# Experts' rows scattered to token order burst by burst, by a row number that each row carries, instead of a gather at the end

## The chip, the cores and the metric

One Trainium2 chip, one core. The metric is the device time of one execution in microseconds, the median of the runs. One core has five engines that run side by side, each through its own list of instructions in order: TensorE (PE), VectorE (DVE), ScalarE (ACT), GpSimd (POOL) and SyncE (SP, which here only issues DMAs). They wait for each other by semaphores.

## What is computed

Input x is 8 batches x 512 tokens x 128. The reference, cut to what matters:

```python
xn = _layernorm(x)
# attention, 16 heads of 8, keys and values through a latent of 64, rope, a mask by pages of 32
q = xn @ wq;  lat = xn @ w_down;  k = lat @ wk_up;  v = lat @ wv_up
s = (softmax(mask(rope(q) @ rope(k) / sqrt(8))) @ v) @ wo
# experts: the two best of 8 for each token
logits = silu(t @ rw1 + rb1) @ rw2 + rb2
vals, idx = top_k(logits, 2)
w = softmax over the two, 0 elsewhere
eh = silu(t @ ew1[e] + eb1[e]);  eo = eh @ ew2[e] + eb2[e]
y = t + sum over e of w * eo
out = x + s * silu(y)
```

All is 32-bit. A token's two expert rows are the only ones that are computed: tokens are sorted into tiles by expert.

## The kernel before

**Attention** goes batch by batch (8), and in a batch by groups of four heads (4), 32 groups in all. For a group SyncE copies the rotated queries and keys into `q_stack` and `k_stack` (`stack`, L515), VectorE and ScalarE mask the keys by head (`k_head`), TensorE computes scores once for their maxima only (L652), VectorE reduces them (`row_max`, L994) and negates them, TensorE turns them (L659), ScalarE copies them to `rows` (`neg_max_t`, L826), and SyncE copies these into spare rows of `q_stack` (L535). Then the scores are computed again with the maximum taken off (L670, L673, L674), in three steps of a group; ScalarE takes the exponentials (`probs`, L845), TensorE multiplies by the values (`pv`, L690, into `wide`), which counts `pv_done`: 12 steps a batch. At a group's end ScalarE copies `wide` to `o_cols` (L852). Behind a batch come transposes (L702, L709), the output projection (L716) and a store to `s_rows`.

**Experts.** The routing (VectorE) gives each token's two places in 39 tiles of 256 rows, sorted by expert. GpSimd scatters the normalised rows `xn` to their places in DRAM (`scatter`, L1175, 64 indirect DMAs of 128 rows, three to a chunk, each chunk held until some step of `pv`). The tiles are then taken in ten bursts of four: SyncE loads expert weights and rows of a tile (`load`, L547 and L549) into a ring of eight, TensorE turns the rows (`slots_in`, L726), ScalarE changes its function table, TensorE and ScalarE compute the first layer (L735, L877), ScalarE changes the table back, TensorE and VectorE compute the second layer (L745, L1112) into `y_out`, and SyncE stores it (`store_rows`, L555) to `y_rows`, in the order of the places. When the last burst is stored, GpSimd gathers each token's two rows (`gather`, L1188, 64 indirect DMAs), VectorE adds them with their weights to `xn` (`combine`, L1124, eight operations a batch), ScalarE takes the gate (`gate`, L883), and VectorE makes the result (`result`, L1135 and L1137) from it, the attention's output and x, which SyncE has fetched again (`fetch`).

**The order of the work** is set by a planner that runs when the kernel is built. `agenda` lists every step with a due place (in groups of attention, from the table AT), its engine, an assumed cost and what it comes after; `program` walks through time and gives each engine the step that can start first among the next LOOK ones of its list. The PSUM banks (7, in `ring`) are given out there as well. The steps' functions then issue their instructions in that order and hold the semaphore waits. GpSimd takes its steps strictly in order of their places.

```python
def chunk(kind, place, first, c, *after):
    add(place, "pool", (kind, c, 0), 1.27 * len(chunk_of(c)), (pv_at(first + c), 0.2), *after)
```

At the start GpSimd makes some constants, computes `rstd` of the first batch (L1162) when VectorE has its variances, and then clears `v_cols` and `pair_in` (L1193, L1194). VectorE normalises the first batch (`norm`, L957) behind `rstd`.

## Time and profile before

| | us |
|---|---|
| median of 3 runs | 509.48 (507.35 to 511.65) |
| the profiled execution | 506.21 |
| its span (first to last instruction) | 504.40 |
| TensorE busy in the span | 439.9 |
| VectorE busy | 375.9 |
| ScalarE busy | 339.1 |
| GpSimd busy | 135.4 |

The profile is of one execution. The span is what lies between its first and last instruction, and the execution is 1.81 us longer. Busy time is added up over the whole span and says nothing of where the engines wait for each other; views of a stretch, the waits and the chain of waits do. A row of the timeline has the start, the duration, engine, line and operation, what is written and read, and in brackets how long the engine had stood idle and what ended that. The matmuls are of 32-bit numbers, and each is shown as two or more instructions.

### The profile page before, as it was taken

To read this page: it belongs to the slowest core of one execution; us is meant where nothing else is said; L and a number is where in the kernel's file an instruction comes from. 1 tells how busy PE (TensorE), PEld (TensorE's weight loads), DVE (VectorE), ACT (ScalarE), POOL (GpSimd) and SP (SyncE) were. 2 spreads that over 40 slices of the span, in tenths; PEclk is the share of its full clock that TensorE was granted. 3 is DMA by queue.
4 is the path that set the end of the run, shared out by engine and by line. 5 is a ranking of instruction groups with operands and counts; after the bars stand their busy time and mean duration, and the time that the engine had idled before them with its cause. 6 is when DMAs were issued, how large, how long until landed. Compare 5 with 4: busy or idle time off the path is not lost.

```text
span 504.4 us, 8192 instructions
## 1 busy us (share of the span) xinstructions
PE 439.9 (87%) x2935; PEld 295.2 (59%) x2935; DVE 375.9 (75%) x721; ACT 339.1 (67%) x537; POOL 135.4 (27%) x143
## 2 busy tenths in 40 slices
PE   2659997989999998999999999999999987998371
PEld 1326654455556556777778876786875743664140
DVE  6788986899888987764658565568468898697751
ACT  2068585656767775788877888787886765665760
POOL 4040000156777750000000000000000377667710
PEclk9858998999999999999999999999999998898787
DMA  6643708122332337655565475466212149335423
GB/s 159 177 122 125 259 24 206 40 75 85 97 97 92 106 97 204 165 153 148 144 183 148 134 188 163 134 179 174 76 43 56 48 116 254 90 79 181 130 65 104
DMA packets 65440, 64.54 MB, mean 128 GB/s; under 512 B 11096, under 2 KB 49112, under 8 KB 64888
## 3 DMA queue, kind: packets, MB, share of 16 engines
q1 hardware_dynamic: 54384, 47.89, 35.0%
q0 software_dynamic: 4096, 8.40, 5.7%
q10 hardware_dynamic: 6920, 7.74, 5.0%
q8 instruction: 23, 0.38, 0.3%
q14 instruction: 17, 0.14, 0.1%
HBM read 32.27 MB, written 21.24 MB: 106 GB/s over the span
## 4 chain that ended last, share of the span: by engine, by line
PE 64%; DVE 11%; DMA 7%; SPq 6%; ACT 6%; issue 4%; POOL 1%; DVEq 0%; POOLq 0%; ACTq 0%
PE ring L652 12%; PE wide L690 12%; PE ring L670 9%; PE ring L745 6%; PE ring L735 6%; DMA q_stack<-rows 4%; DVE row_max L994 4%; ACT probs L845 3%; PE ring L673 3%; PE ring L609 3%; PE ring L702 3%; PE ring L674 2%; PE ring L716 2%; PE ring L726 1%; SPq L546 1%
## 5 line engine op out<-in xcount | busy, mean ns | idle before, releaser
L994 DVE TENSOR_REDUCE row_max<-ring 128x4 f32<-128x512 f32 (+2 forms) x192 | 193.5, 1040 | 50.8 <-PE ring L652 50.1
L845 ACT ACTIVATE probs<-ring 128x768 f32<-128x768 f32 (+1 forms) x192 | 163.0, 880 | 75.6 <-PE ring L670 48.0
L1188 POOL DMA_INDIRECT pair_in<-y_rows,place x64 | 61.7, 964 | 238.8 <-PE wide L690 221.1
L652 PE MATMUL ring<-k_head,q_stack 108*128 108x512 f32 (+1 forms) x352 | 114.5, 420 | 4.3 <-ACT probs L845 2.3
L670 PE MATMUL ring<-q_stack,k_head 128*128 128x512 f32 (+1 forms) x256 | 81.8, 418 | 22.0 <-DMA q_stack<-rows 16.8
L690 PE MATMUL wide<-probs,v_cols 128*32 128x512 f32 (+3 forms) x1024 | 89.6, 449 | 1.3 <-ACT probs L845 1.3
L1175 POOL DMA_INDIRECT slot_rows<-xn,place x64 | 62.3, 974 | 88.8 <-PE wide L690 70.6
L652 PEld LDWEIGHTS ring<-k_head,q_stack 108*128 108x128 f32 x352 | 59.1, 194 | 36.2 <-ACT probs L845 16.9
L670 PEld LDWEIGHTS ring<-q_stack,k_head 128*128 128x128 f32 x256 | 45.3, 202 | 45.4 <-DMA q_stack<-rows 18.9
L837 ACT ACTIVATE k_head<-k_stack,hmask 128x512 fp32r<-128x512 f32 x64 | 43.6, 715 | 6.1 <-DMA k_stack<-roped_lo 6.0
L989 DVE TENSOR_SCALAR k_head<-k_stack,hmask 128x512 fp32r<-128x512 f32 x64 | 29.8, 492 | 21.9 <-DMA k_stack<-roped_lo 21.9
L690 PEld LDWEIGHTS wide<-probs,v_cols 128*32 128x32 f32 x1024 | 24.2, 109 | 34.7 <-issue 23.2
L877 ACT ACTIVATE work<-ring,area 128x256 f32<-128x256 f32 x78 | 30.5, 475 | 11.4 <-PE ring L735 11.4
L745 PEld LDWEIGHTS ring<-area,work 128*128 128x128 f32 x312 | 36.4, 192 | 1.4 <-ACT work L877 0.8
L745 PE MATMUL ring<-area,work 128*128 128x128 f32 x312 | 36.9, 276 | 0.2 <-DVE row_max L994 0.2
L735 PE MATMUL ring<-slots_t,area 128*128 128x256 f32 x156 | 36.6, 384 | 0.1
L673 PE MATMUL ring<-q_stack,k_head 128*128 128x256 f32 x128 | 36.1, 310 | 0.4 <-ACT probs L845 0.2
L673 PEld LDWEIGHTS ring<-q_stack,k_head 128*128 128x128 f32 x128 | 24.2, 189 | 19.2 <-issue 7.3
L735 PEld LDWEIGHTS ring<-slots_t,area 128*128 128x128 f32 x156 | 28.7, 190 | 7.5 <-ACT slots_t L868 2.1
L674 PE MATMUL ring<-q_stack,k_head 128*128 128x256 f32 x128 | 32.4, 281 | 0.0
L762 ACT ACT_TABLE_LOAD x25 | 32.1, 1283 | 0.4
L852 ACT COPY o_cols<-wide 128x512 f32<-128x512 f32 x32 | 18.6, 582 | 12.7 <-PE wide L690 12.0
(131 smaller groups left out, 456.4 us busy)
## 6 DMA issues: line engine op xcount, KB each, us to landing
area<-w_pack SPq DMA_DIRECT2D x39, 321.0 KB, 3.0
area<-slot_rows SPq DMA_DIRECT2D x39, 128.0 KB, 3.1
y_rows<-work SPq DMA_DIRECT2D x39, 128.0 KB, 2.7
k_stack<-roped_hi SPq DMA_DIRECT2D x64, 64.0 KB, 2.0
slot_rows<-pair_in ACTq DMA_DIRECT2D x4, 1024.0 KB, 4.5
q_stack<-roped_hi SPq DMA_DIRECT2D x64, 64.0 KB
k_stack<-roped_lo SPq DMA_DIRECT2D x32, 64.0 KB, 2.0
q_stack<-roped_lo SPq DMA_DIRECT2D x32, 64.0 KB
```

The costliest lines, as they stand in the source:

```text
L652: last = mm(ps[:, k, 0:each * width].rearrange("p (c w) -> p c w", c=each), q_stack[0:MAX0, g, i * P:(i + 1) * P], k_head[0:MAX0, r:r + ea ...
L670: last = mm(ps[:, r, j * P:T], k_head[:, h, j * P:(j + 1) * P], q_stack[:, g, j * P:T], start=True, stop=True)
L673: mm(ps[:, r, 0:2 * P], k_head[:, h, 3 * P:T], q_stack[:, g, 2 * P:T], start=True, stop=True)
L674: last = mm(ps[:, r, 2 * P:T], k_head[:, h, 2 * P:3 * P], q_stack[:, g, 2 * P:T], start=True, stop=True)
L690: last = mm(wide[32 * r:32 * r + 32, dst:T], v_cols[:, tile, GH * g + r, :], probs[:, n % 2, r, src:src + T - dst], start=(tile == 0), sto ...
L735: last = mm(ps[:, c % 2, f * ROWS:(f + 1) * ROWS], w_ring[:, BURST * (burst % 2) + c, f * P:(f + 1) * P], slots_t[:, c * ROWS:(c + 1) * RO ...
L745: last = mm(ps[:, 0, (c % 2) * ROWS + a * E:(c % 2) * ROWS + (a + 1) * E], hidden[:, c, f, a * P:(a + 1) * P], w_ring[:, BURST * (burst % ...
L837: activation(k_head[:, h, :], k_stack[:, g, :], ACT.Copy, scale=hmask[:, r:r + 1]).then_inc(heads_act[g], 1)
L845: activation(probs[:, n % 2, 2 * half:2 * half + 2, lo:T], ps[:, :, lo:T], ACT.Exp, scale=SCALE).then_inc(exp_done, 1)
L994: reduce(row_max[:, g, i, heads[0]:heads[-1] + 1].rearrange("p (a c) -> p a c", c=each), ps[:, :, 0:each * (i + 1) * P].rearrange("p a (c ...
L1175: G.indirect_dma_start(slot_rows, bass.IndirectOffsetOnAxis(ap=place[:, which, t:t + 1], axis=0), xn[:, t, :], None).then_inc(scattered, 16)
L1188: G.indirect_dma_start(pair_in[:, b % 2, which, t * E:(t + 1) * E], None, y_rows, bass.IndirectOffsetOnAxis(ap=place[:, which, at:at + 1], ...
```

## The change

- Each row of `xn` gets a 129th number, the row of `y_rows` to which the expert's result is to go: token number + 9984 (NSLOT) for a token's first expert, and 4096 more for its second. Two iota operations of GpSimd make the numbers. The scatters carry it along: rows are now 516 B, and the order is all first places, then all second ones; between them GpSimd waits until the first 32 scatters have landed and adds 4096 in place.
- The scatters are held for later steps of attention: the first chunk until step 12 (before, 10).
- When a burst's rows are loaded, VectorE takes the maximum of the carried number and the slot's own number (`where`): rows that nobody filled have 0 there and go to their own slot, which nobody reads.
- A burst's results are no longer stored by SyncE but sent by GpSimd (`send`): eight indirect DMAs of 128 rows a burst, 78 in all, to rows in token order. The next burst's second layer waits for them, as it waited for the stores.
- There is no gather. SyncE loads a batch's rows with two plain DMAs of 256 KB (`pairs`), behind the last send.
- The bursts are due 1.553 groups apart instead of 1.0, other places in the table AT are new, LOOK is 28 instead of 16. Two rules are added to the planner: ScalarE's table isn't changed while its held banks leave no pair free, and TensorE starts no other work for ScalarE while the other table is loaded.
- GpSimd clears `v_cols` and `pair_in` ahead of the first batch's `rstd`, not behind it.

```diff
-          pv=0.73, stats=-9.37, route=2.12, scatter=3, burst=(13.14, 1.0), load=0.66, gather=24)
-LOOK, DRIFT = 16, 0.02
+          neg=-0.979, pv=0.862, stats=-9.37, route=3.002, scatter=11 / 3, burst=(12.892, 1.553), load=-0.067,
+          pairs=(30.71, 0.736))
+LOOK, DRIFT = 28, 0.02
...
-                drain_after=[(("sp", ("store_rows", i - 1, 0)), 2.0)] if i else ())
-        add(at + 0.2, "sp", ("store_rows", i, 0), 0.65 * len(tiles), (("dve", ("layer2", i, 1)), 0.1))
+                drain_after=[(("pool", ("send", i - 1, 0)), 2.2)] if i else ())
+        add(at + 0.2, "pool", ("send", i, 0), 2.54 * len(tiles), (("dve", ("layer2", i, 1)), 0.1), (("dve", ("where", i, 0)), 0.1))
...
+            if step[0] == "silu_table" and step[1] < NBURST:
+                kept = {i for other, by in held.items() if by == "act" for i in place[other]}
+                if all({i, i + 1} & kept for i in range(NBANK - 1)):
+                    continue
             if e == "pe" and step in drain:
+                if silu is not None and silu[1] < NBURST and drain[step] == "act" and step[0] != "layer1":
+                    continue
...
-        xn = sb("xn", [P, BT, E])
+        xn = sb("xn", [P, BT, ROW])
...
-        slot_rows = dram("slot_rows", (NTILE * ROWS, E))
-        y_rows = dram("y_rows", (NTILE * ROWS, E))
+        slot_rows = dram("slot_rows", (NSLOT, ROW))
+        y_rows = dram("y_rows", (NSLOT + 2 * B * T, E))
...
-            def store_rows(burst, _):
-                sp.wait_ge(y_ready, 2 * burst + 2)
-                for k in tiles_of(burst):
-                    sp.dma_start(y_rows[ROWS * k:ROWS * k + ROWS, :].rearrange("(a p) d -> p a d", p=P),
-                                 y_out[:, k % BURST, :, :]).then_inc(y_stored, 16)
+            def pairs(b, _):
+                if b == 0:
+                    sp.wait_ge(y_stored, 32 * NTILE)
+                if b >= 2:
+                    sp.wait_ge(mixed, b - 1)
+                for which in range(2):
+                    at = NSLOT + (B * which + b) * T
+                    sp.dma_start(pair_in[:, b % 2, which, :].rearrange("p (t e) -> p t e", e=E), y_rows[at:at + T, :].rearrange(
+                        "(t p) e -> p t e", p=P)).then_inc(pairs_in[b % 2], 16)
...
+            def where(burst, n):
+
+                for k in tiles_of(burst):
+                    dve.wait_ge(w_in_ring[k % W_RING], 32 * (k // W_RING) + 32)
+                count, at = len(tiles_of(burst)), BURST * (burst % 2)
+                if burst >= 2:
+                    dve.wait_ge(y_stored, 32 * BURST * (burst - 1))
+                tt(goes_to[:, at:at + count, :], slots[:, at:at + count, :, E].bitcast(I32),
+                                slot_no[:, BURST * burst:BURST * burst + count, :], ALU.max).then_inc(where_ready, 1)
...
-                pool.wait_ge(pv_done, 3 * AT["scatter"] + c + 1)
-                for t, which in (divmod(k, 2) for k in chunk_of(c)):
+                pool.wait_ge(pv_done, round(3 * AT["scatter"]) + c + 1)
+                for which, t in (divmod(k, BT) for k in chunk_of(c)):
+                    if which and t == 0:
+                        pool.wait_ge(scattered, 16 * BT)
+                        G.tensor_scalar(xn[:, :, E].bitcast(I32), xn[:, :, E].bitcast(I32), BT * P, None, ALU.add).then_inc(named, 1)
+                        pool.wait_ge(named, 2)
                     G.indirect_dma_start(slot_rows, bass.IndirectOffsetOnAxis(ap=place[:, which, t:t + 1], axis=0),
                                          xn[:, t, :], None).then_inc(scattered, 16)
...
-            row_stats(0, 0)
+            def send(burst, n):
+
+                pool.wait_ge(where_ready, burst + 1)
+                pool.wait_ge(y_ready, 2 * burst + 2)
+                for k in tiles_of(burst):
+                    for a in range(2):
+                        G.indirect_dma_start(y_rows, bass.IndirectOffsetOnAxis(ap=goes_to[:, k % W_RING, a:a + 1], axis=0),
+                                             y_out[:, k % BURST, a, :], None).then_inc(y_stored, 16)
+
             G.memset(v_cols[:], 0.0).then_inc(prep_pool, 1)
             G.memset(pair_in[:], 0.0).then_inc(prep_pool, 1)
-            walk("pool", {"stats": row_stats, "scatter": scatter, "gather": gather})
+            row_stats(0, 0)
```

How the instructions stand now. The line numbers of the changed kernel are higher (L826 is L838 there, L845 L857, L852 L864, L883 L895, L762 L774).

ScalarE around the last group of attention, before: `probs` are exponentials, `xn<-xn` the gates, `rows<-ring` the copy of the last maxima.

```order
L845 ACTIVATE probs<-ring 128x1024 x2
L845 ACTIVATE probs<-ring 128x2x384 x4
L762 ACT_TABLE_LOAD
L762 ACTIVATE table_out<-table_in 128x1
L883 ACTIVATE xn<-xn 128x512 x6
L762 ACT_TABLE_LOAD
L762 ACTIVATE table_out<-table_in 128x1
L826 COPY rows<-ring 32x128
L852 COPY o_cols<-wide 128x512
L845 ACTIVATE probs<-ring 128x1024 x2
L845 ACTIVATE probs<-ring 128x2x384 x4
L762 ACT_TABLE_LOAD
```

ScalarE at the same place, changed:

```order
L857 ACTIVATE probs<-ring 128x1024 x2
L857 ACTIVATE probs<-ring 128x2x384
L838 COPY rows<-ring 32x128
L857 ACTIVATE probs<-ring 128x2x384 x3
L864 COPY o_cols<-wide 128x512
L857 ACTIVATE probs<-ring 128x1024 x2
L857 ACTIVATE probs<-ring 128x2x384 x4
L774 ACT_TABLE_LOAD
L774 ACTIVATE table_out<-table_in 128x1
L895 ACTIVATE xn<-xn 128x4x128 x6
L774 ACT_TABLE_LOAD
L774 ACTIVATE table_out<-table_in 128x1
L864 COPY o_cols<-wide 128x512
```

The copy of the last maxima (L838) moved ahead of the six gates and ahead of the three exponentials that end the group before; the gates and both table loads moved behind the last exponentials.

GpSimd at its start, before: `steps` and `tile_no` are constants.

```order
L1152 IOTA steps 128x16
L1154 IOTA tile_no 128x39
L1162 TENSOR_TENSOR rstd<-var_eps,half_exp 128x4
L1193 MEMSET v_cols 128x2048
L1194 MEMSET pair_in 128x2048
L1162 TENSOR_TENSOR rstd<-var_eps,half_exp 128x12
```

GpSimd at its start, changed:

```order
L1174 IOTA steps 128x16
L1176 IOTA tile_no 128x39
L1214 MEMSET v_cols 128x2048
L1215 MEMSET pair_in 128x2048
L1184 TENSOR_TENSOR rstd<-var_eps,half_exp 128x4
L1217 IOTA slot_no 128x78
L1218 IOTA xn 128x32
L1184 TENSOR_TENSOR rstd<-var_eps,half_exp 128x12
```

The two memsets moved ahead of the first `rstd`, and two iota operations came behind it.

TensorE around the last burst of the experts, before: L726 turns the burst's rows, L735 and L745 are its two layers.

```order
L726 MATMUL ring<-ident,area 128x128 x6
L652 MATMUL ring<-k_head,q_stack 128x512 x2
L609 MATMUL ring<-x_col,w_att 128x512
L735 MATMUL ring<-slots_t,area 128x256 x6
L652 MATMUL ring<-k_head,q_stack 128x512 x3
L690 MATMUL wide<-probs,v_cols 32x512 x4
L745 MATMUL ring<-area,work 128x128 x8
L659 MATMUL ring<-ident,neg_max 32x128
L745 MATMUL ring<-area,work 128x128 x4
```

TensorE around the last burst, changed (L738, L747 and L757 are the same three):

```order
L671 MATMUL ring<-ident,neg_max 32x128
L738 MATMUL ring<-ident,area 128x128 x6
L702 MATMUL wide<-probs,v_cols 32x384 x4
L664 MATMUL ring<-k_head,q_stack 128x384 x2
L747 MATMUL ring<-slots_t,area 128x256 x6
L664 MATMUL ring<-k_head,q_stack 128x384 x2
L702 MATMUL wide<-probs,v_cols 32x256 x4
L702 MATMUL wide<-probs,v_cols 32x128 x4
L757 MATMUL ring<-area,work 128x128 x12
L682 MATMUL ring<-q_stack,k_head 128x512 x4
```

The burst itself is the same; before, 1,542 matmuls stand ahead of it, now 1,772, and the transposes of maxima that follow it (L659, now L671) are eight before and four now. Ahead of the first burst stand 778 matmuls before and 786 now.

## Rows read from the trace of the kernel before

**Rows 1.** The page, part 1: busy us, share of the span, instructions
```profile
PE 439.9 (87%) x2935; PEld 295.2 (59%) x2935; DVE 375.9 (75%) x721; ACT 339.1 (67%) x537; POOL 135.4 (27%) x143
```

**Rows 2.** Busy time in stretches; columns: length, each engine, granted clock, DMA share, GB/s
```profile
200.00:400.00 200.00, 198.00 (x1402) 147.77 (x1402) 130.19 (x218) 159.37 (x261) 1.82 (x2) 1.00 0.51 136
400.00:471.00 71.00, 61.81 (x426) 36.84 (x424) 59.31 (x115) 43.29 (x61) 52.04 (x55) 0.93 0.48 134
471.00:479.50 8.50, 0.09 (x2) 0.01 (x1) 7.30 (x16) 5.68 (x12) 6.37 (x8) 0.65 0.60 170
```

**Rows 3.** The page, part 5: groups; busy, mean ns, idle before and its releaser
```profile
L994 DVE TENSOR_REDUCE row_max<-ring 128x4 f32<-128x512 f32 (+2 forms) x192 | 193.5, 1040 | 50.8 <-PE ring L652 50.1
...
L745 PE MATMUL ring<-area,work 128*128 128x128 f32 x312 | 36.9, 276 | 0.2 <-DVE row_max L994 0.2
L735 PE MATMUL ring<-slots_t,area 128*128 128x256 f32 x156 | 36.6, 384 | 0.1
```

**Rows 4.** Timeline of TensorE at 375 us; columns: start us, us, instruction
```profile
375.41 1.06 PE L745 MATMUL ring<-area,work 128*128 128x128 f32 x8
```

**Rows 5.** Waits of 400 to 487 us: us in total, times, longest
```profile
PE ring L670 <- DMA q_stack<-rows: 12.4, 3, 8.4
```

**Rows 6.** Timeline of ScalarE from 470 to 477 us
```profile
469.97 1.28 ACT L762 ACT_TABLE_LOAD   x1
...
471.38 3.21 ACT L883 ACTIVATE xn<-xn 128x512 f32<-128x512 f32 x6
...
476.01 0.24 ACT L826 COPY rows<-ring 32x128 f32<-32x128 f32 x1
```

**Rows 7.** The chain of waits in order of time: start us, us, what
```profile
184.12 2.23 DMA slot_rows<-xn,place
...
194.00 0.44 SPq L549
...
422.23 5.02 DMA q_stack<-rows
...
476.54 2.90 DMA q_stack<-rows
...
486.59 1.28 ACT L762
...
500.96 0.69 DVE area L1137
```

**Rows 8.** Timelines of the start, the normalisations' row to 10.6 and to 10.2 us
```profile
5.41 1.05 POOL L1162 TENSOR_TENSOR rstd<-var_eps,half_exp 128x4 f32<-128x4 f32 x1 [4.02 <-DVE var_eps L950]
...
6.49 4.13 DVE L957 TENSOR_SCALAR xn<-area,mean,rstd 128x128 f32<-128x128 f32 x4 [1.17 <-POOL rstd L1162]
...
6.49 3.87 DVE L957 TENSOR_SCALAR xn<-area,mean,rstd 128x128 f32<-128x128 f32 x3 [1.17 <-POOL rstd L1162]
...
8.16 1.79 POOL L1194 MEMSET pair_in<- 128x2048 f32 x1
```

**Rows 9.** Timeline of GpSimd: the tenth and the last scatter
```profile
115.17 0.96 POOL L1175 DMA_INDIRECT slot_rows<-xn,place  x1 [4.88 <-PE wide L690]
...
184.12 0.96 POOL L1175 DMA_INDIRECT slot_rows<-xn,place  x1 [0.30 <-issue]
```

**Rows 10.** The page, part 6: DMA issues, KB each, us to landing
```profile
area<-slot_rows SPq DMA_DIRECT2D x39, 128.0 KB, 3.1
```

**Rows 11.** Timeline of TensorE: the first burst's transposes
```profile
205.76 1.04 PE L726 MATMUL ring<-ident,area 128*128 128x128 f32 x8
```

**Rows 12.** Groups of VectorE, from 99 to 183 and from 200 to 390 us
```profile
L989 DVE TENSOR_SCALAR k_head<-k_stack,hmask 128x512 fp32r<-128x512 f32 x16 | 7.7, 505 | 0.7 <-DMA k_stack<-roped_lo 0.7
...
L989 DVE TENSOR_SCALAR k_head<-k_stack,hmask 128x512 fp32r<-128x512 f32 x21 | 9.6, 483 | 19.2 <-DMA k_stack<-roped_lo 19.2
```

**Rows 13.** Busy time from 420 to 430 us, columns as in rows 2
```profile
420.00:430.00 10.00, 6.12 (x44) 3.54 (x43) 8.12 (x17) 4.93 (x8) 7.76 (x8) 0.96 1.01 288
```

**Rows 14.** Timeline of VectorE: the first combine
```profile
411.49 2.31 DVE L1124 SCALAR_TENSOR_TENSOR xn<-pair_in,pair_w,xn 128x128 f32<-128x128 f32 x8
```

More of the change, by code:

```diff
@@ L184, in agenda @@
     for c in range(NCHUNK):
-        chunk("scatter", AT["scatter"] + c / 3, 3 * AT["scatter"], c, *([(("dve", ("places", 0, 0)), 0.1)] if c == 0 else []))
-        chunk("gather", AT["gather"] + c / 3, 3 * AT["gather"], c,
-              *([(("sp", ("store_rows", NBURST - 1, 0)), 2.5)] if c == 0 else []),
-              *[(("dve", ("combine", b - 2, 0)), 0.1) for b in range(2, B) if 2 * TT * b in chunk_of(c)])
+        chunk("scatter", AT["scatter"] + c / 3, round(3 * AT["scatter"]), c, *([(("dve", ("places", 0, 0)), 0.1)] if c == 0 else []))
     for i in range(NBURST):
@@ L192, in agenda @@
             add(at - AT["load"] + 0.1 * (k % BURST), "sp", ("load", i, k), 1.3, (("pool", ("scatter", NCHUNK - 1, 0)), 2.5),
-                *([(("pe", ("layer2", i - 2, 1)), 0.2)] if i >= 2 else []))
+                *([(("pe", ("layer2", i - 2, 1)), 0.2), (("dve", ("where", i - 2, 0)), 0.1)] if i >= 2 else []))
+        add(at, "dve", ("where", i, 0), 0.25, *[(("sp", ("load", i, k)), 3.5) for k in tiles])
         job(at, ("slots_in", i, 0), 0.22 * len(tiles) + 0.05, "act", 0.22 * len(tiles) + 0.17,
@@ L211, in agenda @@
     for b in range(B):
-        add(AT["gather"] + last_chunk(b) / 3 + 0.7, "dve", ("combine", b, 0), 2.4, (("pool", ("gather", last_chunk(b), 0)), 2.2),
+        add(AT["pairs"][0] + AT["pairs"][1] * b, "sp", ("pairs", b, 0), 1.3, (("pool", ("send", NBURST - 1, 0)), 2.2),
+            *([(("dve", ("combine", b - 2, 0)), 0.1)] if b >= 2 else []))
+        add(AT["pairs"][0] + AT["pairs"][1] * b + 0.3, "dve", ("combine", b, 0), 2.4, (("sp", ("pairs", b, 0)), 2.5),
             (("dve", ("weights", 0, 0)), 0))
@@ L545, in load @@
                     sp.wait_ge(y_ready, 2 * burst - 2)
+                    sp.wait_ge(where_ready, burst - 1)
                 expert = sp.value_load(tile_e[0:1, k:k + 1], min_val=0, max_val=NE - 1)
@@ L578, in result @@
                 sp.dma_start(out[b].rearrange("(t p) e -> p t e", p=P), s_all[:, TT * b:TT * b + TT, :]).then_inc(stored, 16)
-            walk("sp", {"stack": stack, "neg": maxima, "load": load, "store_rows": store_rows, "s_out": s_out,
+            walk("sp", {"stack": stack, "neg": maxima, "load": load, "pairs": pairs, "s_out": s_out,
                         "fetch": fetch, "result": result})
@@ L801, in norm @@
                 for t in range(TT * b, TT * b + TT):
-                    last = activation(xn[:, t, :], x_all[:, t, :], ACT.Identity, scale=rstd[:, t:t + 1],
+                    last = activation(xn[:, t, 0:E], x_all[:, t, :], ACT.Identity, scale=rstd[:, t:t + 1],
                                       bias=shift[:, t:t + 1])
@@ L1109, in layer2 @@
                 if burst >= 1:
-                    dve.wait_ge(y_stored, 16 * BURST * burst)
+                    dve.wait_ge(y_stored, 32 * BURST * burst)
                 for c in halves_of(burst, q):
@@ L1143, in _ @@
                          "logits": logits, "top": top_two, "gap": gap, "count": count, "ranks": ranks, "places": places,
-                         "weights": weights, "layer2": layer2, "combine": combine, "result": result})
+                         "weights": weights, "where": where, "layer2": layer2, "combine": combine, "result": result})
         @block.gpsimd
```

46 lines of the change are left out of this document (20 added, 26 removed).

## The prediction

> **What bounds the kernel now.** I read the page's shares first: TensorE is busy for 87% of the span, VectorE for 75%, ScalarE for 67% [rows 1]. That averages over stages with different limits, so the next view is the busy time in stretches [rows 2]. From 200 to 400 us, where experts and attention are mixed, TensorE is busy for 198.0 of 200 us: nothing that other engines save there shortens the kernel. Its idle time lies later: 9.2 us between 400 and 471, and all of 471 to 479.5. The experts' two layers are 73.5 us of matmuls [rows 3], and they are used up by 377 us [rows 4]; behind that only attention is left to fill TensorE. The waits of 400 to 487 us name the largest holes: the score matmuls waited three times, 12.4 us together and 8.4 us at the longest, for the copy of the negated maxima into q_stack [rows 5]. ScalarE's timeline tells why [rows 6]: at 469.97 it loads a table, then runs six gates of finished batches, loads the other table, and only at 476.01 copies the last group's maxima (`rows`), behind which SyncE's copy (2.90 us to land, [rows 7]) and the last scores stand.
>
> **The start.** VectorE's four normalisations of the first batch take 4.13 us from 6.49 on, the first three of them 3.87 us, so the fourth adds 0.26 [rows 8]. Beside them GpSimd runs two memsets of 1.79 us, until 9.95. The change issues the memsets ahead of the `rstd` operation that releases the normalisations. GpSimd had stood idle for 4.02 us ahead of that operation [rows 8], from 1.39 to 5.41, so the two memsets (3.6 us) end by 5.0. The four operations should then cost 4 x 0.26 = 1.0 us, and the stage ends 3.1 us sooner. Small operations of VectorE just ahead may meet a memset's end; I charge 0.3 us. Everything up to the first scores hangs on this chain: I take -2.8 us, bounds -3.1 and 0 (if a later load takes over the wait).
> The Trainium skill ("SBUF — State Buffer", section "SBUF: two separate sides") says that a VectorE instruction in a two-port mode and a GpSimd instruction exclude each other for the whole instruction. By that rule the full gain is real, and the trace agrees: of the four, the slow ones lie beside the memsets and the last one, behind them, takes 0.26 us more.
>
> **The rows' scatter.** Of the 64 scatters the last 55 start every 1.27 us from 115.17 to 184.12, behind a 4.88 us wait for TensorE [rows 9]; nine stood ahead of it. The new limits (the 12th step of attention instead of the 10th, then one more step per three scatters) leave three there, so six more come behind 115.17: +7.6 us. Between the halves GpSimd now waits for its DMAs to land, 2.23 us for the last [rows 7], and adds 4096 to the row numbers. No row shows that operation; between nothing and the 1.05 us of `rstd` [rows 8] I take 0.4, and 0.3 for the restart: +2.9 us. The last scatter starts 10.5 us later, 2.8 of it given back by the start: 191.8, landed at 194.1. Before, SyncE had issued the fourth tile's loads 8.1 us behind the landing (184.12 + 2.23 to 194.44, [rows 7]), and they landed 3.1 us later [rows 10]: now 205.3. In TensorE's order the first burst stands behind nearly the same work as before (786 matmuls against 778), so TensorE is there at 205.76 [rows 11] - 2.8 + 0.5 = 203.5. It stands still for 1.8 us; since the landing is a median and the burst needs the fourth tile last, I take +1.5, bounds 0 and +5. Rows of 516 B instead of 512: no row shows such a load; the 3.1 us of the 512 B rows stands, and later loads are issued a burst ahead.
>
> **Stores, gathers, sends.** 39 store issues leave SyncE and 64 gathers leave GpSimd; 78 sends come. At the scatters' 1.27 us the eight of a burst take 10.2 us, and the bursts now stand further apart (ten in some 220 us, 22 us each). A send reads y_out before the next burst's results overwrite it: 10.2 + 2.2 us against 22, so that wait is covered, and if it weren't, VectorE would hold the results and TensorE's banks. Ten `where` operations of 128x8 are each below the 0.69 us of a 128x512 operation [rows 7], on a VectorE that is busy for 130 of 200 us there [rows 2]. Beside DMAs of GpSimd, VectorE's k_head operations take 505 ns, without them 483 [rows 12]: +0.02 us each, hidden too. All at 0; the bounds are 0 and what the third rival costs.
>
> **The spread bursts.** The last burst now stands behind 1,772 matmuls instead of 1,542: four groups of attention are left behind the experts, not eight. A burst is 7.4 us of the two layers (a tenth of 73.5) and 1.0 of transposes [rows 11]. Three of them now lie behind 385 us and fill TensorE's holes up to 430 us, of which 3.9 us lie between 420 and 430 [rows 13] and 1.6 before. I take -5.0 us, bounds -9.2 (all idle time from 400 to 471 us) and 0.
>
> **The last groups.** ScalarE now copies the last maxima ahead of the last group's exponentials, and the gates stand behind all of them. The hole of 8.4 us goes. What is late next is the way behind the last exponentials, which end at 486.6 [rows 7]: table load, the copy of `o_cols`, transposes, projection, store, fetch, the last result, 17.8 us to the end. Now six gates (3.21) and a second table load with its small operation (1.41, from 469.97 to 471.38) stand before that copy [rows 6]: +4.7. VectorE has four results (two operations of 0.69 us each, [rows 7]) ahead of `out_rows`; the first can start 2.0 us behind the exponentials, so they end at about 7.6, as the first transposes do: +0.2. Bounds of this part: -8.4 + 3 and -4 + 7 (if that copy still lands late).
>
> **Sum.** Span 504.4 - 2.8 + 1.5 - 5.0 - 8.4 + 4.7 + 0.2 = 494.6 us. Around the span lie 506.21 - 504.40 = 1.81 us: 496.4. The profiled execution stood 0.65% under the median of the runs (509.48), so 496.4 x 509.48 / 506.21 = **499.6 us**. All bounds at once give spans of some 487 and 512 us, that is 492 and 517 by the same factor.
>
> **Rivals.**
> *Loads collide with the copies of maxima.* One such copy took 5.02 us to land behind a series of 256 KB fetches, another 2.90 [rows 7]. The change puts sixteen loads of 256 KB (`pairs`) into the last 60 us, where 64 gathers had spread the same bytes. If the last batch's four copies each land 3 us later and nothing hides it, 12 us come back: span 506.6, **511 us**. For it: a DMA share of 1.01 from 420 to 430 us [rows 13]. Against: VectorE's maxima run ahead of the copies.
> *The clock stays up.* TensorE's granted clock is 0.93 from 400 to 471 us and 0.65 in the hole behind it, against 1.00 from 200 to 400 [rows 2]: part of the time at the lower of its two levels. If the denser work keeps the upper level, some 5 us (0.07 of 71) and the other 4.2 us of idle time go as well: span 485, **490 us**.
> *The sends are slow, and the kernel slower than before.* They run beside VectorE's work, and each burst's results wait for the previous sends; the 220 us of the bursts leave 2.8 us for each of 78. If each were held up by nearly two of VectorE's reductions (1.04 us, [rows 3]) it took 3.1 us, and they would end at 213 + 242 = 455, land and be loaded by 461. Then VectorE has two combines (2.31 us each, [rows 14]), eleven maxima (1.04) and the negations before the last group can be scored, 17 us; then scores and sums 11, and the tail of 22.7: span 512, **517 us**. It decides from about 2.5 us a send. Against it: the scatters kept 1.27 us beside a VectorE with little idle time.
> The Trainium skill speaks for this rival: "SBUF — State Buffer", section "SBUF: two separate sides", warns that DMAs issued by GpSimd are starved of descriptors while VectorE works in a mode that takes the shared ports, which would put this kernel on this rival's side. The scatters' even spacing doesn't bear that out, so its chance is small.
>
> **How the numbers follow.** Forecast as summed 0.66 (494 to 504 us), clock 0.12, collisions 0.15, slow sends 0.07. One per cent, 5 us, is about what a measurement of this kernel can tell from no change. Faster by over 1% (under 504.4): 0.66 and 0.12, so 0.78. Within 1%: what is between, taken as the collisions, of which some part comes back at nearly every size: 0.15. Slower: 0.07. The range goes from the clock case to the full collisions, 490 to 511 us.
>
> **What would show each step.** The four normalisations at 1.0 to 1.4 us; a gap of some 3 us in the middle of the scatters and a last one near 192; a first burst near 205 us with a short hole ahead; sends every 1.27 us; experts' matmuls until about 425 us; no hole of TensorE over 4 us in the last batch; six gates behind the last exponentials, and some 22.7 us from these to the end. Copies into q_stack that land after 4 to 5 us, or sends over 2.5 us apart, would make the forecast wrong; a first part that is no shorter would take 2.8 us from it.

## The result and the profile after

The changed kernel takes 528.26 us, median of four runs (524.55 to 534.08), the kernel before on the same chip 508.42 (four runs, 506.10 to 511.65): ratio 1.036, 95% interval 1.024 to 1.049. It is slower by 20 us; the forecast was 499.6 and faster. The profiled execution is the longest of the four, 534.08 us with a span of 532.3; counts of waits and places of holes are read from it, times from the medians. Medians are of all runs, ratios leave out runs that lie over 1.5% above the fastest of their kernel, as the profiled one does.

The page of the changed kernel, parts 1 and 6 (to set beside [rows 1, 10]), with the sends' group of part 5:

```profile
PE 458.5 (86%) x2935; PEld 310.5 (58%) x2935; DVE 372.6 (70%) x731; ACT 337.7 (63%) x537; POOL 152.7 (29%) x160
...
L1211 POOL DMA_INDIRECT y_rows<-work,goes_to x78 | 76.6, 982 | 191.7 <-DVE work L1134 170.2
...
area<-w_pack SPq DMA_DIRECT2D x39, 321.0 KB, 3.4
area<-slot_rows SPq DMA_DIRECT2D x39, 129.0 KB, 4.2
```

The load of a tile's rows lands after 4.2 us, where the forecast kept the 3.1 us of the 512 B rows [rows 10]. In the experiments with rows of 516 B it is 3.3 to 4.4 us, in the one with 512 B 3.5, so that the rows' size does it is not shown; and a kernel of the experiments with 3.9 us was as fast as the kernel before, so this isn't the loss.

Busy time in stretches of the changed kernel, columns as in [rows 2]:

```profile
200.00:400.00 200.00, 178.52 (x1170) 127.62 (x1169) 116.02 (x203) 129.44 (x209) 54.81 (x56) 0.93 0.46 129
400.00:471.00 71.00, 67.14 (x476) 49.23 (x475) 44.29 (x69) 52.80 (x86) 21.81 (x22) 0.97 0.36 101
```

TensorE does the same 2,935 matmuls, but from 200 to 400 us, where it had 2.0 us of idle time [rows 2], it now has 21.5, and its granted clock is 0.93 instead of 1.00. The waits of the changed kernel name the place, TensorE's, VectorE's and SyncE's in this order (SPq is SyncE's queue; L682 are the scores, L554 the tile loads, L1134 is layer 2's copy out, L1125 the step `where`):

```profile
PE ring L682 <- DMA q_stack<-rows: 19.7, 8, 4.8
...
DVE work L1134 <- PE ring L757: 33.3, 16, 6.9
...
DVE goes_to L1125 <- DMA area<-slot_rows: 5.9, 3, 2.8
...
SPq L554 <- DVE work L1134: 60.8, 7, 12.6
```

Before, SyncE waited at the loads for layer 2 only 6.2 us in 8 waits; now 60.8 in 7. The kernel before:

```profile
SPq L546 <- DVE work L1112: 6.2, 8, 1.3
```

The chain of waits of the changed kernel from 322 us on shows how one of these waits ends (start us, us, what; four loads follow each other from 325.89 on, the last issue is shown):

```profile
322.36 1.80 PE ring L757 x16
324.19 0.77 DVE work L1134 x2
324.97 0.46 SPq L554
...
325.89 0.35 SPq L555
326.28 0.43 SPq L557
...
331.23 0.44 SPq L557
331.71 4.41 DMA q_stack<-rows
336.17 0.74 PE ring L682 x2
```

Layer 2 of burst i ends; SyncE, which had stood at the first load of burst i+2, issues four tiles' loads (1.65 us a tile); only then comes the copy of the maxima, and it lands 4.41 us later, behind four tiles of 450 KB each. The maxima had been in `rows` since 328.28 us (ScalarE's copy, L838), so 3.4 us went by in SyncE's queue, behind loads that its long wait had pushed to this place. TensorE stands still for 3.2 us meanwhile. The loaded rows are used only some 20 us later. There are holes that end with a copy of maxima at 276, 333, 366 and 389 us (3.0, 3.2, 2.5 and 4.8 us; the copy of the third stood behind six stack copies that the loads had held up), and TensorE pays for them twice. Stretches of the changed kernel around the last of them:

```profile
380.00:389.00 9.00, 8.94 (x62) 4.73 (x60) 8.18 (x13) 5.06 (x9) 5.00 (x6) 1.00 0.64 174
389.00:394.00 5.00, 0.25 (x1) 0.25 (x2) 2.25 (x6) 0.00 (x0) 2.75 (x3) 0.82 0.85 272
394.00:402.00 8.00, 8.00 (x37) 5.12 (x38) 1.63 (x5) 5.44 (x8) 0.00 (x0) 0.69 0.04 9
402.00:410.00 8.00, 8.00 (x56) 6.71 (x56) 3.73 (x5) 6.79 (x14) 0.00 (x0) 1.00 0.01 2
```

Behind the 4.8 us hole the granted clock is 0.69 for 8 us, part of them at the lower of the two levels: TensorE is busy all the time and gets 37 matmuls done where the next 8 us hold 56. The two mixes differ, so the counts alone don't give the price; matmuls of one shape do: the first four score matmuls behind the hole (L682, 128x512) take 670 ns each, where the mean over the kernel is 471, and the next eight value products (L702, 128x512) 951 ns, where it is 639. In this way busy time rises from 439.9 [rows 1] to 458.5 us in the profiled executions with no matmul more; the mean granted clock is 0.917 there, before 0.952.

### The profile page after: what moved, and what is told of

The parts are those of the page before. It is cut to its first block, busy times and chain, and to the rows that moved or that the text cites. A ratio compares the mean times of both kernels' runs of the same rounds, so it can differ in the third digit from the quotient of the medians.

```text
span 532.3 us, 8245 instructions
## 1 busy us (share of the span) xinstructions
PE 458.5 (86%) x2935; PEld 310.5 (58%) x2935; DVE 372.6 (70%) x731; ACT 337.7 (63%) x537; POOL 152.7 (29%) x160
## 4 chain that ended last, share of the span: by engine, by line
PE 56%; SPq 13%; DMA 10%; DVE 8%; ACT 7%; issue 3%; POOL 1%; DVEq 0%; POOLq 0%; ACTq 0%
PE wide L702 10%; PE ring L664 10%; PE ring L682 8%; PE ring L747 7%; PE ring L757 6%; DMA q_stack<-rows 5%; ACT probs L857 4%; DMA k_stack<-roped_lo 4%; DVE row_max L1006 3%; SPq L554 3%; SPq L533 2%; SPq L555 2%; SPq L557 2%; PE ring L621 2%; SPq L530 2%
## 5 line engine op out<-in xcount | busy, mean ns | idle before, releaser
L857 ACT ACTIVATE probs<-ring 128x768 f32<-128x768 f32 (+1 forms) x192 | 161.7, 881 | 73.8 <-PE ring L682 60.1
L1211 POOL DMA_INDIRECT y_rows<-work,goes_to x78 | 76.6, 982 | 191.7 <-DVE work L1134 170.2
L664 PE MATMUL ring<-k_head,q_stack 108*128 108x512 f32 (+1 forms) x352 | 119.4, 435 | 7.6 <-ACT probs L857 3.0
L682 PE MATMUL ring<-q_stack,k_head 128*128 128x512 f32 (+1 forms) x256 | 83.9, 429 | 22.1 <-DMA q_stack<-rows 19.7
L1202 POOL DMA_INDIRECT slot_rows<-xn,place x64 | 64.2, 1002 | 101.9 <-PE wide L702 83.6
L702 PE MATMUL wide<-probs,v_cols 128*32 128x512 f32 (+3 forms) x1024 | 90.7, 453 | 0.9 <-ACT probs L857 0.9
L664 PEld LDWEIGHTS ring<-k_head,q_stack 108*128 108x128 f32 x352 | 62.5, 202 | 43.6 <-ACT probs L857 17.5
L682 PEld LDWEIGHTS ring<-q_stack,k_head 128*128 128x128 f32 x256 | 45.7, 205 | 50.1 <-DMA q_stack<-rows 23.5
L702 PEld LDWEIGHTS wide<-probs,v_cols 128*32 128x32 f32 x1024 | 24.2, 110 | 35.4 <-issue 25.3
L747 PE MATMUL ring<-slots_t,area 128*128 128x256 f32 x156 | 38.0, 396 | 1.0 <-ACT slots_t L880 0.9
L1134 DVE TENSOR_TENSOR work<-ring,area 128x256 f32<-128x256 f32 x39 | 14.8, 419 | 33.6 <-PE ring L757 33.3
L757 PEld LDWEIGHTS ring<-area,work 128*128 128x128 f32 x312 | 36.5, 192 | 3.0 <-ACT work L889 1.6
L757 PE MATMUL ring<-area,work 128*128 128x128 f32 x312 | 37.8, 276 | 0.0
L747 PEld LDWEIGHTS ring<-slots_t,area 128*128 128x128 f32 x156 | 29.9, 197 | 9.1 <-ACT slots_t L880 2.4
L864 ACT COPY o_cols<-wide 128x512 f32<-128x512 f32 x32 | 18.7, 586 | 24.0 <-PE wide L702 23.9
```

The lines of the kernel that those rows point to most:

```text
L664: last = mm(ps[:, k, 0:each * width].rearrange("p (c w) -> p c w", c=each), q_stack[0:MAX0, g, i * P:(i + 1) * P], k_head[0:MAX0, r:r + ea ...
L682: last = mm(ps[:, r, j * P:T], k_head[:, h, j * P:(j + 1) * P], q_stack[:, g, j * P:T], start=True, stop=True)
L702: last = mm(wide[32 * r:32 * r + 32, dst:T], v_cols[:, tile, GH * g + r, :], probs[:, n % 2, r, src:src + T - dst], start=(tile == 0), sto ...
L747: last = mm(ps[:, c % 2, f * ROWS:(f + 1) * ROWS], w_ring[:, BURST * (burst % 2) + c, f * P:(f + 1) * P], slots_t[:, c * ROWS:(c + 1) * RO ...
L757: last = mm(ps[:, 0, (c % 2) * ROWS + a * E:(c % 2) * ROWS + (a + 1) * E], hidden[:, c, f, a * P:(a + 1) * P], w_ring[:, BURST * (burst % ...
L857: activation(probs[:, n % 2, 2 * half:2 * half + 2, lo:T], ps[:, :, lo:T], ACT.Exp, scale=SCALE).then_inc(exp_done, 1)
```

## Experiments

Theories: **A**, SyncE's order (loads that wait hold the copies behind them) makes the loss; **B**, the new path itself costs it (sends, wide rows, traffic); **C**, the new table costs it on all engines. Later ones are D to G. The experiments were run in four groups, so a kernel is best compared by its ratio to the kernel before in its own group. The kernel before, run beside them, had medians of 505.4 to 508.4 us.

**Path and table apart.** New path, positions of before:

```diff
+AT = dict(proj=(-1.9, -1.53, -0.34, 1.77, 2.13, -1.16), router=(0.19, 0.04), heads=-1.71, max=-1.29, max_step=0.12, neg=-1.02,
+          pv=0.73, stats=-9.37, route=2.12, scatter=3, burst=(13.14, 1.0), load=0.66, pairs=(24 + 2 / 3 + 0.7, 8 / 3))
+LOOK, DRIFT = 16, 0.02
```

> The new path alone: GpSimd's scatter with a row number in each row, the sends, wide rows, pair loads and the new start, with the table of positions, the look-ahead of 16 and the burst spacing of 1.0 of the kernel before. Theory A (SyncE's order): near the kernel before, 500 to 512 us, since few copies of maxima stand behind loads that wait. Theory B (the new path itself, by its descriptors, its 516-byte rows or its traffic): 520 us or more. Theory C (table): 500 to 512 us, as A.

Measured 527.81 us, ratio 1.042 (1.034 to 1.049). The other half, kernel before with the new positions, LOOK 28 and the planner's two rules (`burst=(12.892, 1.0)`, `gather=24`):

> The table alone: the kernel before, with its row stores and gathers, by the changed kernel's positions and look-ahead of 28; the bursts keep the spacing of 1.0, since the gathers need the last 84 us. Theory A: 505 to 515 us, as the loads stand between the row stores and are fewer ahead of a copy of maxima. Theory B: 500 to 510 us. Theory C (the positions outside the bursts, such as earlier maxima and later value products, cost it on all engines): 518 us or more.

Measured 508.46 us, ratio 0.999 (0.994 to 1.004). By these two alone the path is guilty and the table (in all but the bursts' spacing, which was left at 1.0) free. But the waits of VectorE in the first (new path, old table) show a wait that the changed kernel hardly has (L1124 is `where` there):

```profile
DVE goes_to L1124 <- DMA y_rows<-work,goes_to: 32.2, 8, 7.5
```

`where` of burst i stands in VectorE's order where its loads are due to have landed, well ahead of the burst's layer 2, and waits for the sends of burst i-2 to land; maxima are queued behind it. So it was moved, alone:

```diff
+def where_late(steps):
+    out = []
+    for s in steps:
+        if s[0] == "where" and s[1] >= 1:
+            continue
+        if s[0] == "layer2" and s[1] >= 1 and s[2] == 0:
+            out.append(("where", s[1], 0))
+        out.append(s)
+    return out
+
+
+ORDER["dve"] = where_late(ORDER["dve"])
```

> The kernel with the new path by the old table (527.8 us), with one step moved on VectorE alone: the step that forms a burst's row numbers stands directly ahead of that burst's first layer 2 copy, not behind its loads. Theory D (the path itself is cheap; what cost 20 us there is that this step waits, in VectorE's queue, for the sends of the burst before last: 32.2 us in 8 waits, and the maxima behind it then come late to TensorE, four holes of 3.5 to 5.6 us ahead of layer 1): 500 to 510 us. Theory B (the path costs by its traffic and its descriptors): above 518 us, with the holes still there or with copies landing late.

Measured 503.11 us, ratio 0.996 (0.993 to 0.999): 24.7 us by the medians, some 23 by the ratios, for one step of 0.16 us in another place. Its TensorE from 200 to 400 us, new path, old table, `where` late:

```profile
200.00:400.00 200.00, 197.38 (x1399) 147.78 (x1396) 130.47 (x229) 157.23 (x257) 75.40 (x78) 1.00 0.49 141
```

All 78 sends lie in this stretch (the x78 of GpSimd), and TensorE is as full as before [rows 2]. Theory B has fallen: the path is free, and so is the table at the old spacing; what each lost was lost by order.

**Copies of maxima first.** In the changed kernel, each `neg` ahead of the run of loads directly before it:

```diff
+        if s[0] in kinds:
+            while at and out[at - 1][0] == "load" and out[at - 1][1] >= 2:
+                at -= 1
+        out.insert(at, s)
...
+ORDER["sp"] = neg_first(ORDER["sp"], ("neg",))
```

> The changed kernel (528 us), with one thing moved on SyncE alone: each copy of maxima that stands directly behind loads of tiles (bursts from the third on) is issued ahead of them (3 to 4 loads, 1.65 us of SyncE each, ahead of 4 copies). Theory A (SyncE's queue costs the loss: loads that wait for layer 2 hold the copies of maxima behind them, in the changed kernel's waits SyncE waited 60.8 us for VectorE at the loads, and TensorE 19.7 us in 8 waits for the copies): the holes of 3.0, 3.2, 2.5 and 4.8 us at 276, 333, 366 and 389 us shrink to 1 us or less, 510 to 520 us. Theory B (the path by GpSimd's sends costs it) and theory C (the table of positions costs it on every engine, not by SyncE): 524 us or more.

Measured 526.63 us (ratio 1.039), a miss for A as it was put. The waits of this kernel point to the reason: TensorE's for the copies fell from 19.7 to 10.6 us, but VectorE's at `where` rose from 7.8 us to 19.7 (13.4 for earlier sends, 6.3 for the rows):

```profile
PE ring L696 <- DMA q_stack<-rows: 10.6, 5, 4.9
...
DVE goes_to L1139 <- DMA y_rows<-work,goes_to: 13.4, 3, 4.9
```

With `where_late` on top:

> As the kernel with the copies of maxima first, and VectorE's step that forms the row numbers of a burst moved down its order to stand directly ahead of that burst's first layer 2 copy, so that VectorE no longer waits for the landing of tile loads (5.9 us in 3 waits in the changed kernel). Theory A: 2 to 6 us below the kernel with the copies first alone, since loads that go out later would otherwise hold VectorE. Theories B and C: the same as that kernel within 3 us.

Measured 521.46 us (ratio 1.031), in the range of A. What was left is shown by the chain of waits of a kernel with the same two moves (it comes below, with four): stack copies (L568, L571) stand behind the loads (L593, L595) as well. ScalarE's k_head (L887) waits for them, behind it in ScalarE's order stands slots_t (L918), which layer 1 (L785) reads, and TensorE has a hole of 4.3 us:

```profile
319.94 0.44 SPq L595
320.47 1.26 SPq L568
...
323.05 0.59 SPq L571
323.68 2.95 DMA k_stack<-roped_lo
326.65 1.33 ACT k_head L887 x2
327.99 0.90 ACT slots_t L918
328.94 6.78 PE ring L785 x16
```

**Loads behind every copy that is due within 10 us**, stack copies too:

```diff
+def loads_later(steps, by):
+    return sorted(steps, key=lambda s: DONE["sp", s] + (by if s[0] == "load" and s[1] >= 2 else 0))
+
+
+ORDER["sp"] = loads_later(ORDER["sp"], 10)
```

With `where_late`:

> The changed kernel with row numbers directly ahead of layer 2 (as before) and, on SyncE alone, every tile load of the third burst on moved behind the stack copies and copies of maxima that the plan puts up to 10 us after it; its rows are needed 20 us later. With the copies of maxima alone ahead of the loads it was 521.5 us, and three holes were left that wait for a stack copy queued behind loads. Theory A (SyncE's queue): those holes go too, 512 to 518 us. If the stack copies are late by the traffic of the loads and not by the queue: 520 to 524 us.

Measured 501.93 us, ratio 0.980 (0.970 to 0.991), 26 us below the changed kernel, faster than the kernel before, and 10 us below the range expected by A: the move did more than close the holes that had been counted. TensorE and SyncE in this kernel: the stretch, TensorE's wait for the maxima (L703), and the head of SyncE's waits, where the loads' wait for layer 2 is no longer found:

```profile
200.00:400.00 200.00, 192.04 (x1342) 139.99 (x1339) 129.30 (x222) 147.20 (x238) 62.62 (x64) 0.98 0.51 138
```

```profile
PE ring L703 <- DMA q_stack<-rows: 6.4, 3, 4.0
...
SPq L563 <- ACT rows L859: 102.9, 24, 12.1
SPq L551 <- PE wide L723: 72.0, 21, 11.4
SPq L593 <- ACT s_sb L895: 18.7, 5, 8.3
```

**Which of the two moves?** Each alone, and half the distance:

> The changed kernel with SyncE's order alone altered: every tile load of the third burst on stands behind the copies that the plan puts up to 10 us after it; VectorE's step for the row numbers stays where it was. With both moves the kernel had 501.9 us. Theory A (SyncE's queue alone made the loss): 502 to 508 us. Theory G (the two orders must move together: a load that goes out later holds VectorE, which waits for its landing to form the row numbers, with the maxima queued behind): 512 us or more, and waits of VectorE at the row numbers for slot rows of over 15 us in all, where it was 5.9 us.

> The changed kernel with VectorE's order alone altered: row numbers directly ahead of layer 2, SyncE's order as in the changed kernel. Theory A: 521 to 527 us, since VectorE waited only 7.8 us there and the holes by the copies of maxima stay. If VectorE's wait was a cause of its own: below 519 us.

> As the kernel of 501.9 us, but the loads stand behind copies that the plan puts up to 5 us after them, not 10. Theory A, if it is the few copies directly behind the loads that matter: half or more of the gain, 505 to 514 us, with waits of SyncE for VectorE at the loads between the 60.8 us of the changed kernel and the few of the kernel with 10 us. If the gain came from something else in the order: no step between, near 502 or near 521 us.

| in the changed kernel: us (ratio) | `where` as it was | `where` late |
|---|---|---|
| loads as they were | 528.26 (1.036) | 526.70 (1.035) |
| loads 5 us later | not run | 516.08 (1.010) |
| loads 10 us later | 542.39 (1.059) | 501.93 (0.980) |

The loads alone make it slower still, by 14 us by the medians and some 12 by the ratios. VectorE's first wait in that kernel:

```profile
DVE goes_to L1133 <- DMA area<-slot_rows: 64.0, 9, 11.5
```

`where` waits for the rows' landing; with the loads later it holds VectorE for 64.0 us, in 9 waits, with maxima behind it. So A alone has fallen, and G holds: the loads stood early on SyncE, `where` stood early on VectorE and wanted their rows there, and one of the two queues pays unless both steps move. With `where` late, 5 us give 10.6 of the 24.8 us. That is a step between, but less than the half or more that was expected, and 2 us above the range. SyncE's waits at the loads, for layer 2 and for `where`, are between as well, 25.7 us:

```profile
SPq L575 <- DVE work L1155: 15.8, 3, 7.0
...
SPq L574 <- DVE goes_to L1146: 9.9, 3, 5.9
```

**Start and end.** The second and third zeroing write moved ahead of the fourth:

```diff
+put(ORDER["act"], ("zero", 1, 0), ("zero", 3, 0))
+put(ORDER["act"], ("zero", 2, 0), ("zero", 3, 0))
```

> The changed kernel with one thing moved on ScalarE alone: the second and third zeroing write, which the new table issues right behind the first at 21 us, stand ahead of the fourth, at some 45 us. Theory E (the three writes of 1 MB together delay the stack copies of batch 0: k_stack<-roped_lo landed 4.3 us after its issue, and TensorE's first value product ended at 71.6 us where it was 67.5 us before and 63.2 us with the old table): first value product at 63 to 66 us and 520 to 523 us in all. If the start was lost by something else: 68 us or later, and the same time as the changed kernel.

Measured 522.96 us (520.22 to 524.83; the changed kernel's runs reach down to 524.55, so the total alone says little). The place does: the first value product ends at 63.2 us, 71.6 in the changed kernel. The chain of waits of the changed kernel shows SyncE's issues of the stack copies, of about 0.6 us, getting slow when three 1 MB writes go out from 21.20 on:

```profile
21.41 0.59 SPq L536
...
22.04 1.20 SPq L537
...
23.29 1.48 SPq L530
...
28.01 1.69 SPq L533
...
29.74 4.29 DMA k_stack<-roped_lo
```

The copy of the last outputs ahead of the table load and the gates:

```diff
+put(ORDER["act"], ("o_copy", B - 1, NG - 1), ("silu_table", NBURST, 0))
```

> The changed kernel with one thing moved on ScalarE alone: the copy of the last attention group's outputs stands ahead of the Silu table load and the six gates, not behind them and a further table load. The hole of 5.8 us in TensorE ahead of the last transposes should go, and the gates come 0.6 us later: if the chain through the output projection sets the end, 521 to 524 us; if the results of the batches (gates, VectorE's products, stores) set it, no change within 1.5 us.

Measured 526.88 us (ratio 1.039), no gain. The first hole went, and another of 7.0 us came behind the first transposes, which this kernel's waits put down to VectorE:

```profile
PE ring L729 <- DVE o_rows L1038: 7.0, 1, 7.0
```

From the last value product to the end it is 24.0 us against 24.8: VectorE's combines and results set the end as much as the gates did.

**Put together.**

> All four moves at once in the changed kernel: copies of maxima ahead of loads, row numbers directly ahead of layer 2, zeroing writes later, last output copy ahead of the gates. If the four losses are separate, 521.5 us (the first two) less 4 to 6 (start) less 4 to 6 (end): 510 to 514 us. If they were all one delay that shows at different places, 518 us or more.

Measured 511.73 us (ratio 1.011, 1.006 to 1.016), as expected if the losses are separate.

> The same with the zeroing writes later and the last output copy ahead of the gates. The kernel with the four moves had 511.7 us. Theory A: 503 to 509 us, as TensorE's holes of 2.7, 4.3, 2.8 and 2.2 us at 296, 325, 353 and 403 us go; what stays above 503 us is the end, where VectorE combines after the last exponentials. If the traffic delays the stack copies: 510 to 513 us.

Measured 499.12 us (495.83 to 499.91), ratio 0.976 (0.967 to 0.985): the fastest kernel of the study, ahead of both, and 4 us below the range expected. Against the kernel of 501.93 us the difference is within the spread of that kernel's runs (496.61 to 507.54). TensorE in it from 200 to 400 us:

```profile
200.00:400.00 200.00, 195.63 (x1360) 143.66 (x1360) 132.20 (x230) 151.60 (x246) 62.63 (x64) 0.99 0.50 136
```

**The spacing.** Theory F: it is the wider spacing of the bursts that costs. Changed kernel with `burst=(12.892, 1.0)`, the old table's pair loads, `where` and zeroing writes late; and the other way round, new path, old table, `where` late with the new spacing, load and pair places:

> The new path with the new table in everything but the bursts' spacing (1.0 for 1.553) and the pair loads' places (those of the old table), zeroing writes later, row numbers directly ahead of layer 2. Theory F (the wider spacing is what puts loads ahead of copies, leaves holes and pushes the combines behind the end): 501 to 507 us. If the other positions of the table (maxima, value products, look-ahead of 28) cost it: 512 us or more.

> The other way round: the best kernel so far (503.1 us, new path, old table, row numbers directly ahead of layer 2) with only the burst spacing of 1.553, the load's place and the pair loads' places of the new table. Theory F: 513 to 520 us, holes between the bursts again and a tail of some 24 us behind the last value product. If the spacing is harmless: 503 to 507 us.

Measured 503.11 us (ratio 0.985, 0.977 to 0.994) and 533.28 us (1.045, 1.036 to 1.055). TensorE's waits for the copies of maxima in the two:

```profile
PE ring L703 <- DMA q_stack<-rows: 8.9, 6, 3.7
...
PE ring L695 <- DMA q_stack<-rows: 21.9, 6, 5.8
```

F holds as a condition: at 1.0 the planner's order leaves few loads in the copies' way, at 1.553 many. The new spacing, with the load's and the pair loads' places that were changed beside it, cost 30 us by the medians and some 25 by the ratios, more than expected. The load's place does no harm by itself, since the first of the two kernels has it too. The spacing isn't a cause by itself either, since 1.553 with the loads later had 501.9 and 499.1 us.

## Why the prediction was wrong

**The step that failed.** "Stores, gathers, sends" ended in "All at 0; the bounds are 0 and what the third rival costs", and of the loads it was only said, under the scatter, that "later loads are issued a burst ahead". That is true, and it is the fault: a load issued a burst ahead waits in SyncE's queue for layer 2, and whatever stands behind it waits as well. In the two holes that were followed, at 333 and 389 us, the copies of the maxima stood 3.4 and 4.4 us in the queue behind such loads and landed 1.5 and 2.2 us later than the 2.90 us of [rows 7]. I counted what leaves SyncE (39 stores), not what the remaining loads stand in front of, in an order that a new table had rearranged. In the same way "Ten `where` operations … hidden" priced their time, below 0.69 us each, and not their waits: with the old table these were 32.2 us and cost 24.7 us of the kernel. No rival held this. The missing term, for both orders together, is +26.3 us by the medians (528.26 - 501.93) and 28 by the ratios, and the bounds of the sum did not contain it.

**The spread bursts** (-5.0). TensorE's holes were not filled but moved: it stood still 21.5 us from 200 to 400 where I had counted on 2.0. The bursts did not keep to 22 us each: their sends start some 27 us apart (from 224.67 to 441.18 us for the first nine). The last layer 2 ended at 458.4 us, forecast "until about 425":

```profile
455.42 2.95 PE L757 MATMUL ring<-area,work 128*128 128x128 f32 x24
```

With both orders mended it ended at 430.6 us (the kernel of 501.9 us) and 420.6 (499.1 us). In the second of these TensorE is idle 4.4 us from 200 to 400 and 7.3 from 400 to 471, together 11.7 where it was 2.0 and 9.2 before, so the term was near 0 even there.

**The start** (-2.8). The operation did as forecast:

```profile
6.37 1.12 DVE L969 TENSOR_SCALAR xn<-area,mean,rstd 128x128 f32<-128x128 f32 x4 [1.17 <-POOL rstd L1184]
```

1.12 us against 4.13 [rows 8]. The rule that the forecast had cited from the Trainium skill ("SBUF — State Buffer", section "SBUF: two separate sides"), that a VectorE instruction in a two-port mode and a GpSimd instruction exclude each other, agrees with this. But a later load took over the wait, the bound of 0 that I had named, and more: the first value product ended 4.1 us later than before (71.6 against 67.5). The new table's three zeroing writes in a row were in the change, and I had not gone through ScalarE's DMAs. With them late it ended at 63.2, 4.3 us ahead of before.

**The rows' scatter** (+1.5) held in its size: a hole of 1.46 us ahead of the first burst (1.8 by the dates, 1.5 taken). Its dates were late: the scatters behind TensorE's wait start at 117.27 us where the forecast had 112.4 (115.17 - 2.8), the last one starts at 197.62 (191.8), and the first burst came at 210.96 us (205). The late start explains 4.9 us of the 5.8 at the last scatter.

```profile
197.62 0.96 POOL L1202 DMA_INDIRECT slot_rows<-xn,place  x1 [0.30 <-issue]
```

In the middle two scatters start 3.26 us apart, so the pause adds 2.0 us to their spacing of 1.27. The forecast added 2.9, since its 2.23 us to land were counted from the start of the last scatter, a part of which the spacing holds already.

**The sends** held: 982 ns each, every 1.27 us within a burst, and the third rival's reason is out, though the kernel is slower, as it said. The Trainium skill's warning ("SBUF — State Buffer", section "SBUF: two separate sides") was set against the scatters' spacing for it. Of these 78 sends beside a VectorE that is busy for 58% of the time from 200 to 400 us none takes over 1.49 us, and the median is 967 ns. The warning is of a mode of VectorE, and no trace here shows which operations ran in it, so this is no test of the warning itself.

**The last groups** (-8.4, +4.7, +0.2). The hole of 8.4 us was gone, and the way behind the last exponentials took 25.7 us (506.57 to 532.3) for the 22.7 forecast. Timeline of ScalarE there:

```profile
505.06 1.51 ACT L857 ACTIVATE probs<-ring 128x768 f32<-128x768 f32 x2 [0.48 <-PE ring L686]
...
507.99 3.21 ACT L895 ACTIVATE xn<-xn 128x512 f32<-128x512 f32 x6
...
512.62 0.57 ACT L864 COPY o_cols<-wide 128x512 f32<-128x512 f32 x1
```

The six gates take the 3.21 us counted, the copy of `o_cols` ends 6.6 us behind the exponentials, as forecast, and VectorE's results end as the first transposes do (515.24 us), as the +0.2 had it. The 3.0 us too much lie behind that. The longer way ahead of the transposes is a hole of 5.8 us in TensorE (1.1 before), and behind it the same 28 matmuls of transposes and projection take 6.86 us for 3.78, at the lower level of the clock throughout. Busy time there, the changed kernel and then the kernel before:

```profile
513.24:522.00 8.76, 6.86 (x28) 5.77 (x28) 7.66 (x15) 2.83 (x5) 0.00 (x0) 0.50 0.49 140
...
488.60:494.00 5.40, 3.78 (x28) 3.12 (x28) 3.73 (x10) 1.71 (x3) 0.00 (x0) 1.00 0.05 15
```

The +4.7 priced ScalarE's operations and not the clock of the matmuls behind them; in this kernel the term measured +7.7.

**The rivals.** "Loads collide with the copies of maxima" named the right victim at the wrong place: between 449 and 507 us TensorE had one such hole, of 1.95 us. The collisions were with the tiles' loads of the middle, which existed before, and the queue ahead of the copy did more than the traffic: 3.4 and 4.4 us against 1.5 and 2.2, as above. (By the forecast's own steps this rival's total comes to 511.7 us, not 511.) "The clock stays up" came true where it looked, 0.97 from 400 to 471 us for 0.93, but the clock fell from 1.00 to 0.93 from 200 to 400, where no rival had looked.

That the fastest kernel, at 499.1 us, meets the forecast of 499.6 us is luck in part: the -5.0 us of the spread bursts was near 0 there too. The forecast left out what stands in front of what, and that kernel has little of it; what its 9 us under the kernel before consist of was not taken apart further.

## What to carry to other kernels

In this kernel a step that waited cost what stood behind it in its queue, not its own time. So for every queue that a change reorders, list each waiting instruction with the three or four instructions behind it and who needs those, before anything is called hidden. Prefetches go behind the short copies that the bound engine needs next, as late as their own use allows; and a step that reads the prefetched data must move with them on its own engine, or the wait only changes queues. When both halves of a change look free or guilty by themselves, look at the waits of each, since two orders can trade the same loss.

## What the runs showed of the hardware that I had not expected

- A hole in TensorE is paid twice: after 4.8 us of standing still the granted clock was 0.69 over the next 8 us, and matmuls of 128x512 took 670 and 951 ns there that take 471 and 639 in the mean of the kernel. After 5.8 us of standing still near the end it was 0.50, and the 28 matmuls that took 3.78 us in the kernel before (granted clock 1.00) took 6.86. TensorE's busy time rose by 18.6 us with the matmuls the same.
- Three 1 MB writes issued by ScalarE within 2.4 us came with slow issues of SyncE's copies, 1.2 to 2.1 us each for the 0.6 otherwise, from 22.04 to 31.8 us, and with a 64 KB copy that landed after 4.29 us. With one such write there (the kernel with the other two late), only the issues from 22.02 to 24.9 us were slow.
- Copies of the maxima landed after 4.41 and 5.05 us behind four tiles of 450 KB, where the last one before took 2.90 [rows 7] and the one ahead of the hole at 366 us, behind six stack copies, 2.58.
